# A four-layer transformer with cross attention: two layers read the context turned, and the second layer runs its cross and self attention as one row of steps

## The reference

```python
x        # (16, 112, 256)
ctx_1024 # (16, 375, 256)
# layer 1 (_L0): parallel attention and feed-forward, then cross attention, 16 heads of 64
# layer 2 (_L1), 16 heads of 16:
x = _layer_norm(x + _mha(x, x, x, *sa, mask), ln1)      # self attention, masked
x = _layer_norm(x + _mha(x, ctx, ctx, *ca), ln2)        # cross attention
x = _layer_norm(x + relu(x @ W1 + b1) @ W2 + b2, ln3)   # feed-forward, 1024 hidden
# layer 3 (_L2): self attention and cross attention with relative position bias, 16 heads of 64
# layer 4 (_L3): a state-space block (convolution of 4 taps, 8 heads, scan), then
#                cross attention over the context, 8 heads of 32, padded keys masked
```

## Time and profile before

| | |
|---|---|
| median of 3 executions | 4230.74 us (4230.36 to 4244.27) |
| the profiled execution | 4239.7 us, span 4238.0 us |
| busy over the span | PE 92%, PEld 75%, DVE 44%, ACT 38%, POOL 8% |
| first layer | about 0 to 1240 us |
| second layer | about 1240 to 2235 us |
| third layer | about 2235 to 3545 us |
| fourth layer | about 3545 to 4238 us |
| HBM read, written | 64.01 MB, 7.40 MB |

### The profile page before, as it was taken

The page is one execution under the profiler, slowest core; times in us unless marked ns, Lnnn a source line. Parts: engine busy times, 40 slices in busy tenths (PEclk is TensorE's granted clock), DMA queues, the critical chain, the costliest instruction groups (busy, mean ns, idle before and its releaser), DMA issues. The chain is left out here.

```text
span 4238.0 us, 68913 instructions
## 1 busy us (share of the span) xinstructions
PE 3909.1 (92%) x23128; PEld 3193.6 (75%) x23128; DVE 1881.8 (44%) x5419; ACT 1614.5 (38%) x3709; POOL 320.5 (8%) x379
## 2 busy tenths in 40 slices
PE   7999999999978999999996999999999997888888
PEld 6888888888867778888774777777777775666666
DVE  3554544545434544555542323323323323546544
ACT  2232333323323433334332454454454443333333
POOL 1000000000001111001100000000000001111110
PEclk9999999999997999999998999999999998899998
DMA  4000000000002000000002000000000000000000
GB/s 167 4 10 13 10 4 13 11 3 13 3 24 94 13 8 12 12 5 12 10 3 75 7 13 7 7 13 7 7 13 7 7 7 21 11 16 16 15 14 5
DMA packets 64014, 75.10 MB, mean 18 GB/s; under 512 B 8336, under 2 KB 61168, under 8 KB 62704
## 3 DMA queue, kind: packets, MB, share of 16 engines
q1 hardware_dynamic: 63728, 71.42, 5.4%
HBM read 64.01 MB, written 7.40 MB: 17 GB/s over the span
## 5 line engine op out<-in xcount | busy, mean ns | idle before, releaser
L313 PEld LDWEIGHTS l_bank<-identity,l_p 112*125 112x125 f32 (+1 forms) x3456 | 516.6, 178 | 244.3 <-issue 18.5
L335 PE MATMUL l_bank<-l_cv,l_pT 125*112 125x65 f32 (+2 forms) x5376 | 640.7, 253 | 54.4 <-ACT l_pT L377 45.4
L161 PE MATMUL l_bank<-l_xT,weights_of_layers_and 128*128 128x224 f32 x3072 | 665.3, 371 | 27.2 <-ACT l_xT L2643 8.5
L335 PEld LDWEIGHTS l_bank<-l_cv,l_pT 125*112 125x112 f32 x5376 | 601.6, 178 | 69.0 <-ACT l_pT L377 32.3
L161 PEld LDWEIGHTS l_bank<-l_xT,weights_of_layers_and 128*128 128x128 f32 x3072 | 595.5, 199 | 55.3 <-ACT l_xT L2643 10.1
L313 PE MATMUL l_bank<-identity,l_p 112*125 112x112 f32 (+1 forms) x3456 | 545.3, 270 | 8.8 <-ACT l_p L366 7.7
L373 ACT ACTIVATE l_p<-l_bank,l_nm 112x375 f32<-112x375 f32 x512 | 293.3, 573 | 487.1 <-DVE l_nm L401 486.6
L303 PE MATMUL l_bank<-l_ckT,l_qz 128*112 128x375 f32 x1024 | 424.3, 498 | 7.2 <-DVE l_qz L1518 7.2
L370 ACT ACTIVATE l_p<-l_p,l_nm 112x375 f32<-112x375 f32 x384 | 233.2, 607 | 470.6 <-DVE l_nm L398 469.2
L366 ACT ACTIVATE l_p<-l_p,l_nm 112x112 f32<-112x112 f32 x768 | 234.8, 376 | 431.8 <-DVE l_nm L394 431.5
L401 DVE TENSOR_REDUCE l_nm<-l_bank 112x1 f32<-112x375 f32 x512 | 279.8, 546 | 204.6 <-PE l_bank L303 201.3
(11 more groups left out here) (244 smaller groups left out, 4859.6 us busy)
## 6 DMA issues: line engine op xcount, KB each, us to landing
l_cx<-in_ctx SPq DMA_DIRECT2D x64, 375.0 KB
x_after_layer<-l_z SPq DMA_DIRECT2D x24, 224.0 KB, 2.4
l_x<-x_after_layer SPq DMA_DIRECT2D x24, 224.0 KB, 2.7
weights_of_layers_and<-in_L_xattn_w_fused SPq DMA_DIRECT2D x1, 2048.0 KB, 9.8
weights_of_layers_and<-in_L_xattn_w_ff SPq DMA_DIRECT2D x1, 2048.0 KB, 12.0
weights_of_layers_and<-in_L_xattn_lin_W SPq DMA_DIRECT2D x2, 1024.0 KB, 11.6
weights_of_layers_and<-in_L_xattn_sa_wkv SPq DMA_DIRECT2D x1, 2048.0 KB, 16.3
weights_of_layers_and<-in_L_xattn_ca_wkv SPq DMA_DIRECT2D x1, 2048.0 KB, 21.2
```

Source lines behind the costliest of these rows:

```text
L161: last = pe.matmul(out, left, right, start=(k == 0), stop=(k == len(pairs) - 1))
L313: last = pe.transpose(bank[:ph.keys, g * T:(g + 1) * T], p[:, m % PD, g * ph.keys:(g + 1) * ph.keys], ident[:T, :T])
L335: last = pe.matmul(bank[:T, g * w:(g + 1) * w], pT[:ph.keys, m % PD, t * T:(t + 1) * T], ph.val(j, r, t), start=(t == 0), stop=(t == ph.ti ...
```

## The change

- The host hands over a second copy of the context, transposed (`ctx_turned`, 16 x 256 x 375). The second and the fourth layer read it, with SP, straight into `cT` (128 partitions, rows of 1500 bytes). Their twelve transposes a turn and ACT's four copies are gone, and with them the jobs `cT`. The next pair's load is issued when the last product that reads `cT` (`cv11`) is done. In the second layer `cT` has SBUF of its own.
- In the second layer the cross phase and the own phase are one call, `[cross, own]`: the own scores follow the cross scores step by step, with no drain between. All side work moves from own steps 0, 1, 4, 5 to 8, 9, 10 to own steps 3, 4, 7, 8 to 10. The own outputs get a buffer of their own (`own.out`).
- The second layer's jobs at the start of a turn are put in another order, and readiness is waited for in smaller parts: scores wait for their own tile of queries and keys, the values for their own sequence's values, the output product `z` for the hidden tiles as it comes to them.
- The first and the third layer are unchanged.

```diff
+def feed_turned(sp, src, cT, come):
+    for j in range(PAIR):
+        sp.dma_start(cT[:, j, :, :], src[j]).then_inc(come.sem, 16)
...
         def own_ready(k):
-            return [P.got(f"v{PAIR - 1}"), P.got("k"), q_spread.this(KT - 1)] if k == 0 else []
+            return [P.got("k"), q_spread.this(k // 2)] if k < own.groups and k % 2 == 0 else []
+
+        def own_values_ready(k):
+            return [P.got(f"v{k // own.groups}")] if k % own.groups == 0 else []
 
         def cross_ready(k):
-            return [P.got(f"cq{KT - 1}"), P.got(f"ck{PAIR - 1}{KT - 1}"), P.got(f"cv{PAIR - 1}1")] if k == 0 else []
+            j, t = k // H, k % H // HEADS_PER_TILE
+            return [P.got(f"cq{t}"), P.got(f"ck{j}{t}")] if k % HEADS_PER_TILE == 0 else []
...
-        beside = {0: [("cOT", "act")], 1: [("u0", "dve"), ("u1", "dve")], 4: [("uT", "act")], 5: [("f0", "act")], 6: [("f1", "act")],
-                  7: [("f2", "act")], 8: [("f3", "act")], 9: [("z0", "dve")], 10: [("z1", "dve")]}
+        beside = {OWN + 3: [("cOT", "act")], OWN + 4: [("u0", "dve"), ("u1", "dve")], OWN + 7: [("uT", "act")],
+                  OWN + 8: [("f0", "act"), ("f1", "act")], OWN + 9: [("f2", "act")], OWN + 10: [("f3", "act"), ("z0", "dve"), ("z1", "dve")]}
...
-                 [("cT00", "act"), ("cT01", "act"), ("OT", "act"), ("cT10", "act"), ("cT11", "act"), ("y0", "dve"), ("y1", "dve"),
-                  ("xT", "act"), ("ck00", "act"), ("ck01", "act"), ("k", "act"), ("ck10", "act"), ("ck11", "act"),
-                  ("q0", "act"), ("q1", "act"), ("v0", "act"), ("v1", "act"), ("cv00", "act"), ("cv01", "act"),
-                  ("yT", "act"), ("cq0", "dve"), ("cq1", "dve"), ("cv10", "act"), ("cv11", "act")]
+                 [("ck00", "act"), ("ck01", "act"), ("OT", "act"), ("ck10", "act"), ("ck11", "act"), ("y0", "dve"), ("y1", "dve"),
+                  ("xT", "act"), ("cv00", "act"), ("cv01", "act"), ("k", "act"), ("q0", "act"), ("q1", "act"), ("v0", "act"), ("v1", "act"),
+                  ("yT", "act"), ("cv10", "act"), ("cq0", "dve"), ("cq1", "dve"), ("cv11", "act")]
...
             def load_context(i, n, views):
-                sp.wait_ge(P.full.sem, P.count_full(i, f"cT{PAIR - 1}{KT - 1}"))
-                feed(sp, None, n, x, cx, xv, views, x_come, c_come)
+                sp.wait_ge(P.full.sem, P.count_full(i, "cv11"))
+                feed_turned(sp, views[n], cT, c_come)
...
+                if s == OWN + 10:
+                    for j in range(PAIR):
...
+                        for f in range(8):
+                            if j == 0 and f == 6:
+                                pe.wait_ge(P.emptier("f3").sem, P.count_emptied(i, "f3"))
...
-                A.tensor(pe, i, [cross], c.ident)
                 if coming:
-                    A.tensor(pe, i, [own], c.ident, lambda s: side(i, s))
+                    A.tensor(pe, i, [cross, own], c.ident, lambda s: side(i, s))
...
-                      8: [("cT00", "act"), ("cT01", "act")], 9: [("ck00", "dve"), ("ck01", "dve")], 10: [("cT10", "act"), ("cT11", "act")],
+                      9: [("ck00", "dve"), ("ck01", "dve")],
...
-        layer1(nc, c, x[0], a["ctx_1024"], x[1], a["mask_SxS_fk0"], weights_of(1), lambda sp: c.l2_weights.issue(sp, "all"))
+        layer1(nc, c, x[0], a["ctx_turned"], x[1], a["mask_SxS_fk0"], weights_of(1), lambda sp: c.l2_weights.issue(sp, "all"))
```

243 lines of the change are left out of this document (103 added, 140 removed), and 2 rows, old and new, of the table state_jobs.

## The result

The changed kernel takes 4212.51 us, the median of 20 executions (4203.07 to 4258.93). The kernel before took 4244.88 us in 20 executions beside them. The ratio is 0.994, with a 95% interval of 0.992 to 0.9961. The forecast was 4213 us.

The account below looks back on a forecast made before the run. TensorE was taken as the bound, through its work, gaps and low clock. Gains of 14.9, 7 and 4 us less 7.8 lost make 18.1 us, from a median of 4230.74 to about 4213 us; range 4187 to 4235.

Parts of the forecast that it names:

- Transposes of the second layer: Second layer's turn start: twelve context transposes fewer gain 1.86 us a turn, 14.9 us in 8 turns.
- The joined row: Second layer's cross and self attention as one row: 43.9 against 44.88 us, 1.0 us a turn, 7 us in 7 turns.
- the 5.2 us of gaps: TensorE's gaps in the second layer's joined section, before own values 0, 3, 4 and 5: 5.2 us instead of 3.52.
- lower end for the seven turns: Worst case for the second layer's joined row, with a clock loss of 7.5 us a turn: -13 us.
- The ends: Second layer's first own row gains 3 us and its last turn about 1: 4 us gained (0 to 5).
- The fourth layer: Fewer transposes there win 1.4 us but lose cover between gaps, and more low clock costs 9.2: net 7.8 us lost.
- change nothing that anyone waits for: Context loads: rows of 1500 bytes instead of 1024 were said to delay or speed nothing.
- The fourth layer's clock does not care: Rival: wider gaps in the fourth layer cost no clock, so 9.2 us are not lost; 4204 us, chance 0.15.
- No gain from the transposes: Rival: second layer's keys wait as long as the transposes took, so 14.9 us are missing; 4228 us, chance 0.08.
- The own row keeps its clock: Rival: second layer's own row loses 1.7 us to clock, not 4.5, 20 us more gained; 4193 us, chance 0.25.
- low throughout: Rival: second layer's own row stays at low clock until the hidden products, losing 7.5 us; 4234 us, chance 0.12.
- The anchor: The kernel before was taken at 4230.74 us, the median of three runs, as the level for the forecast.

Follow-up runs that it names:

- the run with the rows apart: The changed kernel with cross and self attention of the second layer as two rows of steps again, side work at its old own steps: 4221.09 us, ratio 0.9988.
- the idle transposes: The changed kernel with six transposes of a weight tile, results unread, at each of the fourth layer's steps 8 and 10: 4203.83 us, ratio 0.9916.
- the keys in its gaps: The changed kernel with the second layer's context keys moved beside own steps 5 to 7, one context value product in their place: 4161.73 us, ratio 0.9811.
- both moves: The changed kernel with second-layer context keys beside own steps 5 to 7 and fourth-layer first keys and values at steps 8 to 10: 4141.49 us, ratio 0.9751.

## Why the prediction was right, and which terms were not

- **Transposes of the second layer**: 14.9 us forecast. From the first of these transposes to the first cross transposes it was 25.50 us (1557.19, to 1582.69) and is 23.38 (1551.41 to 1574.79): 2.1 us a turn, 17 in 8 turns, where 1.86 was the transposes' own time. The start's jobs also stand in another order; no run separates the two. By the means of seven turns the kernel before has 115.3 us, its code in the run with only the fourth layer changed 113.8, and the run with the rows apart 113.0. By their difference (114.6 - 113.0) this part is worth only 1.6. That fits the layer better: 17 + 7 + 7 us would be 31, and it gained 27.
- **The joined row**: 1.0 us a turn forecast and 1.0 measured, by the mean over seven turns against the run with the rows apart. The places in the reasoning were right: the clock stays up over the junction and falls behind the gap at own values 3. The terms were not. The forecast had the joined row 1.2 us longer as a schedule, "all it can win is clock", with a clock loss smaller by 6.7 - 4.5 = 2.2 us. The run with the rows apart shows the reverse: 1.8 us shorter as a schedule, and a clock loss that is 0.7 to 1.0 us larger. The step that failed is the 5.2 us of gaps: the section of the turn above has 42.08 - 39.13 = 2.95 us of them (2.43 at the two places). And the run with the rows apart loses less clock than I took for it, since every other of its turns keeps 0.98. That the two errors cancel to the forecast's 1.0 us is luck. (The forecast's lower end for the seven turns, given as -13 us, comes out as -14.)
- **The ends**: 4 us forecast, about 7 measured (3 in the first own row, 4 in the last turn, where I had put 1).
- **The fourth layer**: 7.8 us lost forecast, 6 measured as a mean over traces that overlap. The mechanism is the forecast's: slow keys in five turns of seven were forecast, six or seven came. Its start gained 4.2 us that the forecast excluded. The step that failed there is its sentence that rows of 1500 bytes instead of 1024 "change nothing that anyone waits for". At the start of that layer someone does. In 2 us in the middle of the load the kernel before and the changed one show, by windows:

```profile
3560.00:3562.00 2.00, 0.00 (x0) 0.00 (x0) 0.00 (x0) 0.00 (x0) 1.63 (x7) 0.50 0.33 117
```

```profile
3525.00:3527.00 2.00, 0.00 (x0) 0.00 (x0) 0.00 (x0) 0.00 (x0) 1.85 (x6) 0.55 1.00 307
```

The transfer ran at 117 GB/s with 0.33 of the 16 DMA engines busy, which is 5.3 of them, and now runs at 307 with all 16. Per busy engine that is 22 and 19 GB/s, so the longer rows did not make an engine faster; more engines work. The load has 128 partitions instead of 125. The Trainium skill, "DMA: Bandwidth & Descriptors", section "Why a DMA increments its semaphore by 16 and not by 1", says that a transfer is spread over the largest number of engines, at most 16, that divides its outer size on both sides. An estimate by that rule gives 5 engines for 125 partitions, and the section has 16 for 128. The two busy shares agree with it. No run here changes the number of partitions alone.

- **The rivals.** "The fourth layer's clock does not care" is refuted by the idle transposes and by the count of slow keys. "No gain from the transposes" is refuted by the turn's start. "The own row keeps its clock" and "low throughout" did not happen in the changed kernel; with the keys in its gaps the first did, and the layer gained 53 us where the rival had put 20: the clock loss that goes is about 6 us a turn, not 2.8. A clock that stays low throughout does occur, but in the cross attention, where I had not looked, and there it costs 50 us at a time.
- **The anchor.** Three runs of the kernel before (4230 to 4244) were taken for its level; 20 put it at 4244.9. The range held it; a gain of 18 us on the right level would have read 4227.

## What to carry to other kernels

Before work is taken from the bound engine, look at what stands next to its gaps: work in a thin stretch is cover, and taking it away (the fourth layer) can cost more than it took, while moving needed work there (keys and values into the gaps) gave 71 us (4212.5 to 4141.5) where the whole change, with twelve transposes a turn removed from each of two layers, gave 32. Where the granted clock differs between turns of one trace, compare the means of all turns of several executions, never one turn with one turn: a single pair gave 2.8 us here for a thing that is worth 1.0. And plot the single times before trusting a median: half of the executions in an upper group moved it by 23 us.

## What the runs showed of the hardware

- The low clock can outlast the gaps ahead of it. From 1448.60 to 1554.40 in the trace with both moves PE is busy without a pause and stays at 0.50, through a whole cross attention; the same instructions in the next turns run at 1.00. It came back behind the products of `u`, the row's side work (1.45 us for scores at 1553.39, 0.94 at 1558.39, against 1.70 before).
- The length of a gap alone does not tell whether the clock falls. Gaps of 1.00 us (before own values 0) never cost it in the six turns with the keys in the gaps, and did in one of the changed kernel's seven; 1.43 us at own values 3 always did there, and 0.63 and 0.92 us at the join did in two turns of seven.
- Transposes whose results nobody reads kept the clock over the products behind them: slow first keys in 0 of 7 turns against 34 of 35 without them, and the layer took 670.4 us against 673.9 to 680.1.
- Two loads of 375 KB in 125 partitions moved at 117 GB/s with 5.3 of 16 DMA engines busy, and the small loads behind them in the same queue came 3.5 us later; in 128 partitions they moved at 307 GB/s with all 16.
